# Three PSUM banks in turn for transposed weights in a deformable convolution with experts

## What is computed

```python
def block(x):
    z = layernorm(x)                                   # over the 64 channels
    x_proj = z @ w_in + b_in                           # the image to be sampled
    x1 = gelu(layernorm(depthwise3x3(z)) * g + b)
    offset = (x1 @ w_off).reshape(B, H, W, 8, 9, 2)    # 8 groups, 9 taps, (x, y)
    mask = softmax((x1 @ w_mask).reshape(B, H, W, 8, 9))
    samp = bilinear(x_proj, tap position + offset)     # four corners each
    x = x + sum(samp * mask over the 9 taps) @ w_out
    t = layernorm(x)
    top2 of softmax(x @ Wr); y_e = gelu(t_e @ W1_e + b1) @ W2_e + b2   # 8 experts, 256 hidden
    return x + weighted sum of the top two y_e
```

## Time and profile before

| | |
|---|---|
| median of 3 runs | 317.01 us (316.65 to 318.73) |
| profiled execution, its own time | 316.45 us |
| its span in the trace | 314.7 us |
| PE, PEld busy | 280.6 us (89%), 181.6 us (58%) |
| DVE, ACT, POOL busy | 240.7 us (76%), 259.7 us (83%), 119.7 us (38%) |
| prologue; stages 0, 1, 2, 3; tail | 31.28; 59.33, 68.14, 67.43, 63.82; 24.7 us |

### The profile page before, as it was taken

The page is one execution under the profiler, slowest core; times in us unless marked ns, Lnnn a source line. Parts: engine busy times, 40 slices in busy tenths (PEclk is TensorE's granted clock), DMA queues, the critical chain, the costliest instruction groups (busy, mean ns, idle before and its releaser), DMA issues.

```text
span 314.7 us, 8541 instructions
## 1 busy us (share of the span) xinstructions
PE 280.6 (89%) x3307; PEld 181.6 (58%) x3307; DVE 240.7 (76%) x720; ACT 259.7 (83%) x505; POOL 119.7 (38%) x122
## 2 busy tenths in 40 slices
PE   7896999978799998899989998899878999998895
PEld 2462566635467764445667663355666788676562
DVE  6979869998957987769887887498958354479565
ACT  3789778898797899999797999988868899887473
POOL 5200142503552515022493504050875713569230
PEclk9969999997999999999999999999999999999999
DMA  6910000000000000000000000000000000000000
GB/s 150 296 39 0 2 2 4 0 2 0 2 3 2 3 3 0 0 2 3 2 9 13 0 2 1 2 2 1 2 19 0 3 2 2 10 1 11 0 2 17
DMA packets 7190, 4.84 MB, mean 15 GB/s; under 512 B 5090, under 2 KB 6831, under 8 KB 7087
## 3 DMA queue, kind: packets, MB, share of 16 engines
q1 hardware_dynamic: 7150, 4.31, 5.6%
HBM read 2.04 MB, written 0.52 MB: 8 GB/s over the span
## 4 chain that ended last, share of the span: by engine, by line
PE 44%; ACT 22%; DVE 15%; POOL 9%; issue 8%; DMA 1%; DVEq 0%; ACTq 0%; POOLq 0%
ACT wk L1276 5%; PE zl_ps L1522 5%; ACT wk L1271 4%; PE zh_ps L1519 4%; PE ga_ps L1553 4%; PE ga_ps L1555 3%; PE ga_ps L1554 3%; PE m_ps L1655 3%; DVE prod L855 3%; ACT dl L1257 2%; PE m_ps L1638 2%; ACT h_all L1307 2%; POOL prod L546 2%; PE m_ps L1622 2%; PE m_ps L1624 2%
## 5 line engine op out<-in xcount | busy, mean ns | idle before, releaser
L855 DVE TENSOR_TENSOR prod<-ga_ps,wx 128x480 f32<-128x480 f32 x96 | 61.9, 651 | 31.5 <-PE ga_ps L1555 30.7
L546 POOL TENSOR_TENSOR prod<-prod 128x960 f32<-128x960 f32 (+1 forms) x20 | 39.8, 1990 | 115.8 <-DVE prod L855 115.8
L1271 ACT ACTIVATE wk<-zh_ps 128x512 f16<-128x512 f32 x108 | 65.3, 605 | 22.4 <-PE zh_ps L1519 21.3
L1553 PE MATMUL ga_ps<-v_all,wk 128*128 128x80 f16 x576 | 79.8, 202 | 4.1 <-DVE prod L855 2.2
L1555 PE MATMUL ga_ps<-v_all,wk 128*128 128x80 f16 x576 | 79.8, 202 | 0.0
L1554 PE MATMUL ga_ps<-v_all,wk 128*128 128x80 f16 x576 | 79.8, 202 | 0.0
L1553 PEld LDWEIGHTS ga_ps<-v_all,wk 128*128 128x128 f16 x576 | 57.0, 99 | 17.5 <-issue 7.5
L1276 ACT ACTIVATE wk<-zl_ps 128x512 f16<-128x512 f32 x108 | 65.5, 607 | 0.0
L1554 PEld LDWEIGHTS ga_ps<-v_all,wk 128*128 128x128 f16 x576 | 57.4, 100 | 8.1 <-issue 0.3
L1555 PEld LDWEIGHTS ga_ps<-v_all,wk 128*128 128x128 f16 x576 | 57.6, 100 | 0.0
L1522 PE MATMUL zl_ps<-tab,sel_lo 128*128 128x512 f16 x108 | 41.9, 388 | 7.0 <-ACT wk L1276 4.4
(11 more groups left out here) (282 smaller groups left out, 624.4 us busy)
## 6 DMA issues: line engine op xcount, KB each, us to landing
v_all<-still SPq DMA_DIRECT2D x1, 1440.0 KB, 9.7
h_all<-in_W SPq DMA_DIRECT2D x1, 512.0 KB
w_s<-in_W SPq DMA_DIRECT2D x1, 512.0 KB
x_tok<-in_x SPq DMA_DIRECT2D x1, 384.0 KB, 6.6
out_dram<-x_tok SPq DMA_DIRECT2D x6, 64.0 KB, 2.0
w_high<-w_high SPq DMA_DIRECT2D x1, 256.0 KB, 2.9
const<-in_table SPq DMA_DIRECT2D x1, 218.0 KB, 2.7
vec<-in_vectors SPq DMA_DIRECT2D x1, 132.5 KB
```

The costliest lines, as they stand in the source:

```text
L546: then(pool.tensor_tensor(p[:, 0:3, :], p[:, 0:3, :], p[:, 3:6, :], ALU.add))
L855: dve.tensor_tensor(prod[q % 2][:].rearrange("p k n -> p (k n)")[:, f * PB * NV:(f + 1) * PB * NV] .rearrange("p (n c l) -> p n c l", n=PB ...
L1271: act.activation(wk[n % WR][:, 0, :], zh_ps[:], ACT.Relu, scale=W_SCALE).then_inc(s_wkh, 1)
L1553: pe.matmul(to, w_h, high, start=True, stop=False)
```

## The change

`m_ps[1]` joins `zh_ps` and `zl_ps` in a ring of three for stages 0 to 2: half 2n (high) and 2n + 1 (low) of unit n go to bank (2n) mod 3 and (2n + 1) mod 3. So the high product waits for the low copy of unit n - 2, the low product for the high copy of unit n - 1. For chunks 0 and 1 the steps behind the gather all use `m_ps[0]`; expert_in takes `m_ps[0]` and `m_ps[2]` in turn, expert_out `m_ps[3]` alone, and outputs_t banks 0, 2, 3, 2. The last stage keeps its banks. In the prologue POOL builds 10 of the 18 rows of `sel_lo`, in one instruction, FILL has one and four more zero products at two points (ahead of project and of image_t), and DVE's `input_stats(1)` comes behind the column weights. The five distances become single steps, and nearly all places in the lists are new. In the stage without experts behind it (0), the bias products are all issued by place 1.5, and three pairs of zero products stand at other places.

```diff
+SEL_POOL = 10
...
-            "bias_product": [0, 0, 0, 0, 4.5, 4.5, 4.5, 5.5], "zeros": [19.5, 22.5, 19.5]}
...
+            "bias_product": [0, 0, 0, 0, 0, 0, 0.5, 1.5], "zeros": [19, 22, 22.5]}
...
-PE_MIDDLE = {"input_t": 0, "convolve": [4, 6, 7, 7], "project": 5, "image_t": [9, 12.5], "conv_t": 14, "offsets": 15.5,
-             "table": [33.5, 35.5], "samples_t": 3, "project_out": 4.5, "experts_t": 8, "router": 11,
-             "expert_in": [12, 13, 13.5, 13.5, 16.5, 16.5, 18.5, 18.5, 19.5, 21, 22.5, 23, 24.5, 25, 27, 28],
-             "expert_out": [17.5, 21.5, 26, 31.5], "outputs_t": [33.5, 34.5], "b2": 35}
-ACT_MIDDLE = {"pad_image": 0.5, "project_high": 5.5, "image_out": 11.5, "conv_gelu": 14.5, "tap_exp": 16.5,
-              "distances": 21, "samples_out": 4, "zn_out": 9.5, "router_exp": 16.5,
-              "hidden": [12.5, 12.5, 14.5, 15, 17.5, 18, 18.5, 19.5, 21.5, 22, 22.5, 23.5, 26.5, 26.5, 27.5, 28.5],
-              "outputs_out": [20, 30.5, 31, 32.5]}
...
+PE_MIDDLE = {"input_t": 0, "convolve": [6, 7, 7, 7.5], "project": 6, "image_t": [9, 13.5], "conv_t": 15, "offsets": 16,
+             "table": [34.5, 35.5], "samples_t": 4, "project_out": 5.5, "experts_t": 8, "router": 11.5,
+             "expert_in": [18, 19, 20, 20, 20.5, 21, 21.5, 22, 23, 23.5, 24.5, 24.5, 27, 27, 28, 29],
+             "expert_out": [23, 24.5, 30, 31], "outputs_t": [34, 35.5], "b2": 35}
+ACT_MIDDLE = {"pad_image": 0, "project_high": 6, "image_out": 12.5, "conv_gelu": 15, "tap_exp": 17.5,
+              "distances": [22.5, 22.5, 23, 23, 24], "samples_out": 4.5, "zn_out": 9, "router_exp": 16.5,
+              "hidden": [18.5, 19.5, 20, 20, 21, 21.5, 22, 22.5, 23, 23.5, 24.5, 25.5, 27, 28, 30.5, 30.5],
+              "outputs_out": [23.5, 26.5, 30.5, 33]}
...
-FILL = [9, 2, 8, 9, 7, 6, 2]
...
+FILL = [9, 2, 9, 13, 7, 6, 2]
...
+        z_ring = [zh_ps[:], zl_ps[:], m_ps[1]]
+        z_ps = [zl_ps, zh_ps]
+
+        def high_ps(unit):
+            return z_ring[2 * unit % 3]
+
+        def low_ps(unit):
+            return z_ring[(2 * unit + 1) % 3]
...
+            return m_ps[bank if d >= LAST - 1 else 0]
...
+            return m_ps[n % 2 if d >= LAST - 1 else 2 * (n % 2)]
...
+            return m_ps[2 + t] if d >= LAST - 1 else m_ps[((0, 2), (3, 2))[i][t]]
...
+                pool.wait_ge(s_selc, 1)
+                pool.tensor_tensor(sel_lo[:, 0:SEL_POOL, :], sel_own[:, 0:SEL_POOL].unsqueeze(2).to_broadcast([P, SEL_POOL, KC]),
+                                   coef_lo[:].unsqueeze(1).to_broadcast([P, SEL_POOL, KC]), ALU.mult).then_inc(s_sel, 1)
...
             hats(0)
+            tap_weights(0)
+            column_weights(0)
             dve.wait_ge(s_x_rest, N_X)
             input_stats(1)
-            tap_weights(0)
-            column_weights(0)
...
-            for f in range(FW):
+            for f in range(SEL_POOL, FW):
...
+                    pe.wait_ge(s_y_rd, 2 * (a - 3) + 1)
+                transposes(xn, m_ps[0]).then_inc(s_xnT, 1)
+
+            def convolve(a, t):
+
+                pe.wait_ge(s_xpad, a + 1)
+                if a == 1 and t == 0:
+                    pe.wait_ge(s_bias, 2)
+                if a > 2 and t == 0:
                     pe.wait_ge(s_y_rd, 2 * (a - 2))
-                transposes(xn, m_ps[0]).then_inc(s_xnT, 1)
...
             def weights_t(j, n):
                 q, k = n // K2, n % K2
+                pe.wait_ge(s_wkl, units_done(j, n) - 1)
+                pe.matmul(high_ps(units_done(j, n)), sel_hi[:, 2 * k:2 * k + 2, :].rearrange("p g m -> p (g m)"), tab[j % 2][:, q, :],
+                          start=True, stop=True).then_inc(s_zh, 1)
                 pe.wait_ge(s_wkh, units_done(j, n))
-                pe.matmul(zh_ps[:], sel_hi[:, 2 * k:2 * k + 2, :].rearrange("p g m -> p (g m)"), tab[j % 2][:, q, :],
-                          start=True, stop=True).then_inc(s_zh, 1)
-                pe.wait_ge(s_wkl, units_done(j, n))
-                pe.matmul(zl_ps[:], sel_lo[:, 2 * k:2 * k + 2, :].rearrange("p g m -> p (g m)"), tab[j % 2][:, q, :],
+                pe.matmul(low_ps(units_done(j, n)), sel_lo[:, 2 * k:2 * k + 2, :].rearrange("p g m -> p (g m)"), tab[j % 2][:, q, :],
                           start=True, stop=True).then_inc(s_zl, 1)
...
-                if 0 < d < LAST:
+                if d < LAST - 1:
+                    pe.wait_ge(s_xpad, d + 3)
+                if d == LAST - 1:
...
-                if n == 1:
+                if n == (0 if d < LAST - 1 else 1):
                     pe.wait_ge(s_lg_rd, d + 1)
+                if n == 1 and d < LAST - 1:
...
-                    pe.wait_ge(s_ysb, copies_before(d) + m - 1)
+                    pe.wait_ge(s_ysb, copies_before(d) + m)
                 for a in range(HC):
                     for r in range(2):
-                        ins = pe.matmul(m_ps[2 + m % 2][r * C:(r + 1) * C, :], w2_s[:, (2 * m + r) * HC + a, :],
+                        ins = pe.matmul(m_ps[3][r * C:(r + 1) * C, :], w2_s[:, (2 * m + r) * HC + a, :],
...
+                    if d < LAST - 1 and (i, t) == (1, 1):
+                        pe.wait_ge(s_y_rd, 2 * d + 1)
```

More of the change, by code:

```diff
@@ L47 @@
 ONE = 7 * FW
+SEL_POOL = 10
 FINE = 2.0 ** 10
 ROUND = 1.5 * 2.0 ** 23
-PE_FIRST = {"input_t": 3.5, "convolve": [7, 8.5, 9, 9.5], "project": 6.5, "image_t": [10, 11.5], "conv_t": 14.5,
-            "offsets": 15.5, "table": [23, 27], "samples_t": 12, "project_out": 8, "experts_t": 12.5, "router": 10,
-            "expert_in": [10, 20, 26.5, 44.5, 47.5, 54, 56.5, 71, 74, 92.5, 101, 105.5, 108.5, 112, 113.5, 122],
-            "expert_out": [11.5, 11.5, 13.5, 17, 19, 20.5, 23, 24], "outputs_t": [17, 25.5], "b2": 15,
-            "bias_product": [0, 0, 0, 0, 4.5, 4.5, 4.5, 5.5], "zeros": [19.5, 22.5, 19.5]}
@@ L90 @@
-ACT_LAST = {"pad_image": 8, "project_high": 9, "image_out": 1.5, "conv_gelu": 24.5, "tap_exp": 23.5, "distances": 27.5,
-            "samples_out": 3.5, "zn_out": 11.5,
-            "hidden": [18.5, 18.5, 20, 21.5, 25.5, 27, 29, 30, 30.5, 35, 36.5, 38.5, 41, 44.5, 44.5, 46.5],
-            "outputs_out": [32.5, 48], "half_samples_out": 48.5, "half_zn_out": 57.5}
+PE_FIRST = {"input_t": 4, "convolve": [7.5, 9, 9, 9], "project": 7, "image_t": [11, 12], "conv_t": 15, "offsets": 16.5,
+            "table": [23.5, 30], "samples_t": 12, "project_out": 8, "experts_t": 12.5, "router": 10,
+            "expert_in": [9, 12.5, 21, 37, 37.5, 44, 46.5, 61, 64, 81.5, 91, 92.5, 95.5, 102, 103, 111.5],
+            "expert_out": [11.5, 11.5, 13.5, 17, 19, 20.5, 23, 24], "outputs_t": [17, 25.5], "b2": 14,
+            "bias_product": [0, 0, 0, 0, 0, 0, 0.5, 1.5], "zeros": [19, 22, 22.5]}
@@ new lines @@
+POOL_MIDDLE = {"tap_tree": [19.5, 21.5, 23, 29], "combine": [31.5, 34.5], "conv_rstd": 21, "inner_rstd": 7,
+               "input_rstd": 22}
+PE_LAST = {"input_t": 7.5, "convolve": [4.5, 9, 15.5, 21], "project": 0, "image_t": [11.5, 25], "conv_t": 24.5,
+           "offsets": 13.5, "table": [37, 27], "samples_t": 3.5, "project_out": 5.5, "experts_t": 11, "router": 17,
+           "expert_in": [19.5, 19.5, 20, 22, 24, 27.5, 29, 29, 31.5, 35, 36, 36.5, 40, 40.5, 43.5, 46],
+           "expert_out": [22.5, 26, 32, 32, 44.5, 44.5, 46.5, 48], "outputs_t": [38.5, 55.5], "b2": 25,
+           "half_samples_t": 48.5, "half_project_out": 50.5, "half_experts_t": 58, "half_router": 61.5, "zeros": [9, 10.5]}
@@ L113 @@
 HALF_FQ = FQ // 2
[L115 to L120 removed]
+TAIL = {"samples_t": 4, "project_out": 5, "experts_t": 7, "router": 9,
+        "samples_out": 3, "zn_out": 6, "outputs_out": 10, "outputs_t": 11}
+FILL = [9, 2, 9, 13, 7, 6, 2]
 FIRST = -(-6 * TP // PB)
@@ L370, in outputs_by_token @@
         def outputs_by_token(d, i, t):
-            return m_ps[(0 if i == 1 and d < LAST - 1 else 2) + t]
+            return m_ps[2 + t] if d >= LAST - 1 else m_ps[((0, 2), (3, 2))[i][t]]
         def x2(d):
@@ L1376, in body @@
                             zn_out(LAST, 0)
-                    if has_a and n == at["distances"]:
-                        distances(j + 1)
+                    if has_a:
+                        for l in range(LOC):
+                            if n == at["distances"][l]:
+                                distance(j + 1, l)
                     if has_d:
```

157 lines of the change are left out of this document (81 added, 76 removed).

## The result

| | before | after |
|---|---|---|
| median of 11 runs each, side by side on one chip | 316.65 us (316.04 to 318.73) | 320.24 us (316.34 to 320.56) |
| ratio | | 1.0093, 95% interval 1.0071 to 1.0115 |
| profiled execution, span | 316.45, 314.7 us | 320.56, 318.7 us |

The change makes the kernel 0.9% slower (1.1% by the medians); 308.0 was forecast, and 320.24 lies above the range. One of its eleven executions took 316.34 us. To place the 4 us I cut both traces at the start of ACT's first high copy of each stage, and the last stage at its last copy of weights. The halves are units 0 to 17 and 18 to 35.

The account below looks back on a forecast made before the run. No engine alone was the bound: PE, ACT and DVE wait for each other. From 316.45 us: prologue -1.2, short steps -1.2, stage 0 -2.8, stages 1 and 2 -6.4, bank +2.6, giving 307.4 (308.0 by the median); range 303 to 317.

Parts of the forecast that it names:

- What pays for the third bank: Stages 1 and 2: experts sharing fewer banks wait near places 23 and 31, charged 1.3 us a stage, +2.6 in all.
- rival C: Stages 1 and 2: experts pressed into second halves, 2.9 us of ACT moved, +8.2; kernel slower, 321.2 us; chance 0.15.
- The waits of stages 1 and 2, -6.4: Stages 1 and 2: PE begins later work up to one copy earlier, cutting ACT's waits by 3.2 us each.
- Stage 0, -2.8: Stage 0: the ring cuts ACT's 8.4 us of waits for high products by a third, 2.8 us.
- rival B: DVE becomes the bound: stages 1 and 2 give 1 us each, stage 0 nothing; 313.8 us; chance 0.12.
- The short steps, -1.2: 23 steps between units shrink 0.10 us each from about 1.08 us, 2.3 us at most, 1.2 taken.
- Stage 3, 0 within 1.5: Stage 3 and tail: two banks stay and only places move, so 0, bounds -1.5 and +1.5 us.
- The prologue, -1.2: Prologue: GpSimd's ten rows save ACT 2.4 us, of which 1.2 is gained; bounds 0 and -2.4.
- rival D: Clock kept in the prologue and most waits regained, 1.2 + 3 us more than forecast: 303.8 us; chance 0.11.
- The features that the sum let bind at 27.46 us: Prologue: DVE's features end only at 27.46 us, so the table copy starts at about 28.05.
- The stretch of sel_hi that I feared: Prologue: GpSimd's rows stretch DVE's 1.36 us sel_hi by up to 1.9, losing up to 0.9 us on first positions.
- What I said would show C: Sign of rival C: ACT's waits for PE grow more in units 18 to 35 than they fall in 0 to 17.

Follow-up runs that it names:

- experiment 3: The changed kernel, same banks and places, but each high or low product waits for the same-half copy of the unit before, removing PE's lead: 332.18 us, ratio 1.0456.
- experiment 5: Experiment 2 with the changed kernel's late places for expert and outputs steps in stages 1 and 2, old banks, no ring: 328.92 us, ratio 1.0396.
- experiment 1: The changed kernel with stage 0's five distances together at place 22, as before, instead of four at 19.5 and one at 21: 319.06 us, ratio 1.0058.
- experiment 4: The changed kernel's prologue and stage 0 with ring, distances at 22; stages 1 to 3 as in the kernel before: 315.18 us, ratio 0.9945.
- experiment 6: Experiment 1 with eight more zero products at place 3 of the last stage: 317.36 us, ratio 1.0023.
- experiment 2: The kernel before with only GpSimd's ten sel_lo rows and the longer FILL in the prologue: 314.22 us, ratio 0.9920.
- experiment 7: The kernel before with only FILL changed, one and four more zero products in the prologue: 316.60 us, ratio 0.9997.
- experiment 11: The kernel before with GpSimd's ten sel_lo rows and old FILL, leaving out half the columns of stage 2's 16 hidden activations: 313.30 us.
- experiment 10: Experiment 6 with stages 1 and 2's experts begun earlier, the first four expert_in on m_ps[0] alone from place 14, DVE's first routing step at 12: 330.72 us, ratio 1.0428.
- experiment 12: Experiment 6, leaving out half the columns of stage 2's 16 hidden activations: 315.18 us.

## Why the prediction was wrong

**The step that failed: "What pays for the third bank", 2.6 us.** I charged the late experts two local waits a stage, at places 23 and 31. Without the lead, the new places and banks cost 10.8 us over the two stages (experiment 3), and the late places of the experts alone, with the rest as before, 14.7 (experiment 5, which keeps the distances in their midst). They move 3.8 us of ACT's and 3.2 us of PE's work into 18 units in which each waits for the other. What the shared banks cost apart from the places was not separated. I had this mechanism as rival C and its first figure (2.9 us moved) was near; but I had it only as an alternative, and let the forecast stand as if the moved work cost nothing. That C's 321.2 lies beside the measured 320.24 is luck: C had +8.2 for stages 1 and 2 and -2.8 for stage 0, and they came out as +1.9 and +2.6.

By the runs, then, stages 1 and 2 pay 10.8 us where the sum had 2.6, the lead gives back 8.9 where it had 6.4, and the rest of the miss lies in stage 0 and in the clock of stage 3.

**The waits of stages 1 and 2, -6.4.** At the new places the lead gives 8.9 in these stages (experiment 3), more than this. But the sum set it against a kernel whose places hadn't moved, and there PE was busy 63.4 of 68.1 us, which stood in the earlier trace rows: by that row about 4.7 us of PE's idle time was to be had in stage 1, if every other wait went too. I asked for 3.2 of that and then for 0.1 us at each short step. In the event ACT's waits for products fell by 1.4 in stage 1 and others rose by 2.4. Ring and price together are +1.07 and +0.84 instead of -1.9 for each stage (3.2 less 1.3).

**Stage 0, -2.8.** It came out +2.6. About 2 of that is the place of the distances (experiment 1), which I hadn't priced at all: I read the moved places as following the ring. The lead by itself is worth 2.6 us here at the new places (experiment 3), near the 2.8; but ring and places together gave nothing (experiment 4). What takes it back was only read from the trace: PE's gathers wait for DVE and its column weights, which is rival B for this stage (5.7 us in experiment 4, 2.2 before). "The short steps, -1.2" are seen: 19 steps between the high copies of stage 0 are 0.97 to 1.05 us long, where before none was under 1.06. They are lost again before the stage ends.

**Stage 3, 0 within 1.5.** +2.2, and outside of its bounds. Nearly all of it is the clock behind one wait of 2.10 us (experiment 6). I gave this stage bounds for its places and no term for a clock that can fall. The same wait is 1.57 us in the kernel before, and in seven profiled executions with it the clock fell in two (experiments 2 and 7); at 1.9 to 2.1 us it fell in two of three (the changed kernel and experiment 1, not experiment 3), with the extra zeros in none of four.

**The prologue, -1.2.** It gave 2.6, rival D's part. In the trace the granted clock is 1.00 over the whole prologue, and the product that took 3.22 us takes 1.70. By the rule of the Trainium skill (TensorE: Matmul & The Clock Gate, "What's actually happening"), which I had weighed and left out of the sum, activity keeps the array fast; experiment 7 agrees, with 1.70 us where FILL alone was changed. But experiment 11 kept the clock with the old FILL, so one execution is no proof; eleven without a fall against one of three are the evidence. The features that the sum let bind at 27.46 us were done at 25.93 in the changed kernel, and ACT's whole 2.4 us came through.

The stretch of sel_hi that I feared didn't come: 1.36 us with GpSimd's rows beside it and without. This doesn't speak against the contention: GpSimd started second here, at 17.86 against DVE's 17.81, and its own instruction took 2.43 us against my 1.9, under cover all the same. In the rows of the kernel before, the one that starts second is the one that gets longer. In the earlier trace rows that is DVE; in stage 1 it is GpSimd, whose tree step takes 3.58 us where the one at 58.59 us takes 2.22:

```profile
153.54 1.65 DVE L843 TENSOR_TENSOR wx<-dl,mask 128x1440 f32<-128x1440 f32 x1
153.70 3.58 POOL L546 TENSOR_TENSOR prod<-prod 128x960 f32<-128x960 f32 x1 [9.74 <-DVE prod L855]
```

The rule of the Trainium skill (GPSIMD Engine Reference, "Specifications") names the contention, and these rows agree with it; I had read it as if it always fell on DVE.

What I said would show C, ACT's waits rising in units 18 to 35 by more than they fall in 0 to 17, wasn't what happened: they rose in the first half by 1.3 us and fell in the second by 0.1. The half grew by its work.

**What stays open.** What a ring would be worth with a bank of its own can't be tried, as the kernel has taken all eight. Nor was it tried whether the new places of the front steps (2.4 us of new waits in stage 1) could be mended. That a slow stretch goes when PE's pause is filled rests for the last stage on counts of executions and on the medians of experiments 1 and 6; for the prologue on the counts above. With the distances at 19.5 (the changed kernel and experiment 3) a fall stands at 65.4 and 69.2 us; with them at 22 three of five profiles have none before 79.8, but two have one at 71.1 (experiments 10 and 12), so there the clock isn't settled. The stretch at 82.4 us has no such test, and at 191.6 us there is no pause to fill.
